# Moving a layer stack's prologue into the setup of a conditioned sequence kernel, with a shorter QR step and a tail spread over other phases

## The reference

```python
# L0: rotation
U, _ = jnp.linalg.qr(P)                      # P: 288 x 64
v = silu(cond) @ W.T + b                     # 2016 values a sample
A = skew matrix 64 x 64 from v;  R = expm(A)
z = einsum('btn,nd->btd', x, U)
x = x + einsum('btd,nd->btn', z @ R - z, U)
# L1, L2, L3: each with its own weights
s_a, c_a, g_a, s_f, c_f, g_f = split(silu(cond) @ W_ada + b_ada, 6)
h = layernorm(x) * (1 + c_a) + s_a
x = x + g_a * (softmax(q k^T / sqrt(18)) v @ W_proj + b_proj)   # 16 heads, q, k, v = h @ W_qkv + b_qkv
h = layernorm(x) * (1 + c_f) + s_f
x = x + g_f * (gelu(h @ W_fc1 + b_fc1) @ W_fc2 + b_fc2)         # 288 -> 1152 -> 288
```

## Time and profile before

| | us |
|---|---|
| median of three runs (lowest, highest) | 2118.55 (2117.92, 2121.7) |
| the profiled execution | 2125.66 |
| its span | 2123.9 |
| TensorE busy | 1966.4 (93%) |
| VectorE busy | 1224.8 (58%) |
| ScalarE busy | 1107.5 (52%) |
| GpSimd busy | 1015.8 (48%) |

### The profile page before, as it was taken

The page is one execution under the profiler, slowest core; times in us unless marked ns, Lnnn a source line. Parts: engine busy times, 40 slices in busy tenths (PEclk is TensorE's granted clock), DMA queues, the critical chain, the costliest instruction groups (busy, mean ns, idle before and its releaser), DMA issues. The chain is left out here.

```text
span 2123.9 us, 50051 instructions
## 1 busy us (share of the span) xinstructions
PE 1966.4 (93%) x16599; PEld 1746.1 (82%) x16599; DVE 1224.8 (58%) x2813; ACT 1107.5 (52%) x1906; POOL 1015.8 (48%) x1045
## 2 busy tenths in 40 slices
PE   4684599999999999999999999999999999999997
PEld 2553378998989988879989999888789899998986
DVE  7766375565655665574655556575656565565641
ACT  2222346656465564556465564654664655646552
POOL 2002164555545554655545545455645455454544
PEclk9887689999999999999999999999999999999998
DMA  6604243333233333343233333333432333333320
GB/s 167 160 13 142 83 135 107 95 89 99 80 108 91 93 95 95 111 131 100 80 104 88 98 99 84 99 88 93 144 96 81 103 88 99 99 83 100 86 80 25
DMA packets 138669, 207.65 MB, mean 98 GB/s; under 512 B 35204, under 2 KB 95778, under 8 KB 137518
## 3 DMA queue, kind: packets, MB, share of 16 engines
q1 hardware_dynamic: 111742, 171.06, 28.9%
q10 hardware_dynamic: 24192, 27.94, 4.7%
q0 software_dynamic: 2640, 7.44, 1.2%
HBM read 99.81 MB, written 20.82 MB: 57 GB/s over the span
## 5 line engine op out<-in xcount | busy, mean ns | idle before, releaser
L1968 DVE TENSOR_REDUCE maxima<-scores 128x4 f32<-128x1024 f32 x384 | 460.7, 1222 | 185.7 <-PE scores L1718 180.9
L1294 POOL TENSOR_TENSOR hidden<-g_full,hidden 128x512 fp32r<-128x512 f32 (+1 forms) x240 | 280.5, 1177 | 356.8 <-ACT hidden L1544 355.8
L1501 ACT ACTIVATE probs<-scores 128x1024 f32<-128x1024 f32 x384 | 383.2, 1026 | 95.2 <-PE pv_ps L1755 57.1
L1780 PE MATMUL mlp_ps<-h_mlp,w_up 128*128 128x256 f32 (+1 forms) x3024 | 405.6, 287 | 8.2 <-ACT hidden L1544 4.7
L1780 PEld LDWEIGHTS mlp_ps<-h_mlp,w_up 128*128 128x128 f32 (+1 forms) x3024 | 377.5, 191 | 42.0 <-issue 19.3
L1635 PE MATMUL mlp_ps<-w_down,hidden 128*128 128x288 f32 x2592 | 388.1, 294 | 0.0
L1635 PEld LDWEIGHTS mlp_ps<-w_down,hidden 128*128 128x128 f32 x2592 | 368.9, 188 | 18.5
L1718 PE MATMUL scores<-k_stack,q_stack 108*128 108x512 f32 x768 | 241.9, 407 | 22.4 <-DMA k_stack<-qk 18.4
L1741 PE MATMUL scores<-q_stack,k_stack 110*128 110x256 f32 x1536 | 246.5, 293 | 3.3 <-ACT probs L1501 2.0
L1741 PEld LDWEIGHTS scores<-q_stack,k_stack 110*128 110x128 f32 x1536 | 207.8, 191 | 32.1 <-issue 18.9
L1491 ACT ACTIVATE neg_max<-att_ps 16x256 fp32r<-16x256 f32 x48 | 18.0, 375 | 387.7 <-PE att_ps L1728 387.7
(11 more groups left out here) (221 smaller groups left out, 2865.9 us busy)
## 6 DMA issues: line engine op xcount, KB each, us to landing
q_stack<-qk SPq DMA_DIRECT2D x144, 180.0 KB
k_stack<-qk SPq DMA_DIRECT2D x288, 90.0 KB
inv_sum<-inv_scratch ACTq DMA_DIRECT2D x192, 128.0 KB, 2.7
k_stack<-qk SPq DMA_DIRECT2D x288, 54.0 KB
x_in<-out_x SPq DMA_DIRECT2D x48, 288.0 KB, 3.8
x_mid<-out_x SPq DMA_DIRECT2D x48, 288.0 KB, 4.2
out_x<-x_out SPq DMA_DIRECT2D x48, 288.0 KB, 3.1
q_stack<-qk SPq DMA_DIRECT2D x144, 72.0 KB
```

The source lines that it names most:

```text
L1294: tt(out, full, high.bitcast(F32), ALU.subtract).then_inc(signal, 1)
L1501: evict(probs[:, u % 4, :, :, :], scores[u % 2][:, :, :, :], ACT.Exp, scale=SCALE)\
L1780: last = mm(up_bank[n % 2][:, (m % 2) * T:(m % 2 + 1) * T], w[:, m * P:(m + 1) * P], h, start=count == 0, stop=count == 6)
L1968: nc.vector.tensor_reduce(out=maxima[:, :, :, u], in_=scores[u % 2][:, :, :, :], axis=AX.X, op=ALU.max).then_inc(s_max, 1)
```

## The change

The layers' tiles that the prologue writes are allocated first, and the setup (now called `prepare`) is called from within `layers` after them, with the tiles and semaphores handed over as `early`. What the prologue did is distributed over the setup: ScalarE fills `v_sb` and `k_stack` in phases 0 and 1 and rounds a third of `w_in` in each of phases 6, 7 and 8; GpSimd stages `w_in` after the skew loads; VectorE forms the low parts in the tail and the statistics and normalisation of sample 0, which it now adds into `x_in` directly, between the later adds. The wait for the stores moves from the end of the setup to the layers' SyncE program.

In the QR step `size` is gone: `pivot` is sign * alpha + norm with sign = +-0.5 in one instruction, with the scales of `mask`, the square roots and `norm_col` halved to fit. `turn` and `recip` share a semaphore, `factor` and `update` another. `recip` comes behind `update`. In a change, `spread` comes ahead of `norm_col`. Pair 1 goes into phase 3, pairs 2 and 3 into phase 4, one pair each into 5 to 8; the high powers go into phase 3 and the series and squarings forward; modulation set 0 goes into phase 8, set 1 to where set 0 was, set 2 behind the third pair's differences. The skew stores and loads are shared by SyncE and GpSimd, w_rot is loaded earlier, the constants and the first x group go over ScalarE's queue. Of `w_ada` two layers are held instead of three.

```diff
 (rotation_setup becomes prepare(nc, dram, keep, early))
-        SQUARES = {5: range(0, 6), 6: range(6, 15), 7: range(15, 24), 8: range(24, FILLS)}
-        PAIRS = {2: (0,), 4: (1, 2), 5: (3,), 6: (4,), 7: (5,), 8: (6,), PHASES: (7,)}
-        POWERS_AT, SERIES_AT = 3, 4
+        SQUARES = {5: range(0, 8), 6: range(8, 17), 7: range(17, 26), 8: range(26, FILLS)}
+        PAIRS = {2: (0,), 3: (1,), 4: (2, 3), 5: (4,), 6: (5,), 7: (6,), 8: (7,)}
+        POWERS_AT = 3
...
+        def skew_store(engine, q, half):
+            engine.wait_ge(s_v, q + 1)
+            for i in (2 * half, 2 * half + 1):
+                n = TILES * q + i
+                engine.dma_start(dram["v_scratch"][:, n * SKEW_COLS:(n + 1) * SKEW_COLS],
+                                 v_rot[32 * i:32 * i + B, q, :]).then_inc(s_v_st[half], 16)
+        def skew_load(engine, q, half):
+            for stored in s_v_st:
+                engine.wait_ge(stored, 32 * (q + 1))
+            rows = slice(R // 4 * q, R // 4 * (q + 1))
+            engine.dma_start(a_raw[half * R + rows.start:half * R + rows.stop, :, :], a_view[half, rows]).then_inc(s_a_ld[half], 16)
...
         @block.sync
+            for q in range(4):
+                skew_store(sp, q, 0)
+                skew_load(sp, q, 0)
+            sp.wait_ge(s_skew_ps, 4)
+            sp.wait_ge(s_a_ld[0], 64)
+            sp.wait_ge(s_a_ld[1], 64)
...
             for l in range(L):
+                if l == 2:
+                    sp.wait_ge(s_rows_ps, 1)
...
             sp.wait_ge(s_gates_st, 16 * TILES)
-            sp.wait_ge(s_out_st, 16 * B)
...
         @block.gpsimd
+            for q in range(4):
+                skew_store(pool, q, 1)
+                skew_load(pool, q, 1)
+            pool.wait_ge(s_x[2], 16)
+            for n in range(3):
+                early["stage"](pool, 0, n)
...
         @block.scalar
             for k in range(PHASES):
                 if k == 0:
+                    constant_stacks()
                     skew_out(0)
                 if k == 1:
+                    constant_rows()
                     skew_out(1)
                     skew_out(2)
+                    a, b = GROUPS[0]
+                    act.dma_start(x_all[:, a:b, :, :], dram["x"][a:b].rearrange("s p t c -> p s t c")).then_inc(s_x[0], 16)
...
+                if k in (6, 7, 8):
+                    high_weights(k - 6)
+                if k == LAST:
+                    mod_rows_out(0)
+                    mods_out(0)
                 if k < LAST:
                     norms(k)
...
         @block.vector
-                    V.tensor_scalar(size[h, i % 2:i % 2 + 1], alpha, -1.0, alpha, ALU.mult, ALU.max).then_inc(s_size, 1)
                 V.tensor_scalar(sign[h, n:n + 1], alpha, 0.0, 0.5, ALU.is_ge, ALU.subtract).then_inc(s_sign, 1)
...
-                V.tensor_tensor(pivot[h, n:n + 1], size[h, i % 2:i % 2 + 1], norm[h, n:n + 1], ALU.add).then_inc(s_pivot, 1)
+                dve.wait_ge(s_sign, n + 1)
+                V.scalar_tensor_tensor(out=pivot[h, n:n + 1], in0=alpha, scalar=sign[h, n:n + 1], in1=norm[h, n:n + 1],
+                                       op0=ALU.mult, op1=ALU.add).then_inc(s_pivot, 1)
...
-                dve.wait_ge(s_turn, n + 1)
-                dve.wait_ge(s_recip, n + 1)
+                dve.wait_ge(s_ratio, 2 * n + 2)
...
                 for i in range(WIDE):
-                    sign_and_size(k, i)
+                    sign_and_pivot(k, i)
...
-                    pivots(k, i)
                     turned(k, i)
-                    inverse_pivot(k, i)
                     if i:
                         update(k, i - 1)
+                    inverse_pivot(k, i)
                     factors(k, i)
...
                 whole_columns(k)
-                column_norms(k)
                 fill(k, GAP_A)
                 spread_rows(k + 1)
+                column_norms(k)
                 fill(k, GAP_B)
...
+            low_weights(0)
             dve.wait_ge(s_c_ps, 1)
...
+            rotated(0)
+            rotated(1)
+            for t in range(2):
+                V.bn_stats(out=stats[:, t, :], in_=x_in[:, t, :]).then_inc(early["s_stats"], 1)
+            rotated(2)
+            for t in range(2):
+                V.bn_aggr(out=mean_var[:, t, :], in_=stats[:, t, :]).then_inc(early["s_var"], 1)
+            for s in range(3, 8):
+                rotated(s)
+            (four tensor_scalar that write x_hat)
+            for s in range(8, B):
+                rotated(s)
...
 layers, block.sync
-            sp.dma_start(x_in[:, :, :], dram["out"][0]).then_inc(s_xin, 16)
+            sp.sem_inc(s_xin, 16)
+            sp.wait_ge(s_out_st, 16 * B)
+            sp.sem_inc(s_x_st, 16 * B)
...
 layers, block.vector, prologue
-                attention_norm(0)
-                x_hats(0, 0, x_in, s_xhat_a)
-                convert_weights(0, OF["w_in"], "qk")
-                convert_weights(0, OF["w_in"], "v")
-                (four tensor_scalar that write the last rows of k_stack)
                 for n in range(QK_USES):
                     qk_low(0, n)
```

477 lines of the change are left out of this document (247 added, 230 removed).

## The result

| | median us | lowest to highest | runs |
|---|---|---|---|
| before | 2119.69 | 2117.92 to 2121.7 | 4 |
| after | 2102.99 | 2097.45 to 2105.64 | 4 |

The ratio is 0.9918 (95% interval 0.9895 to 0.9940): 16.7 us faster, where 31.6 were forecast. 2087.0 and the whole range 2077 to 2098 were too low.

A forecast was written before the change was run, and what follows sets the result against it. It took a serial chain before the first query/key products as the bound. Gains of 15.4 (prologue), 2.5 (boundary), 2.8 (differences), 6.5 (tail) and 4.4 (QR) made 31.6, off the median 2118.55: 2087.0 us, range 2077 to 2098.

The forecast's parts named there:

- The start needs neither `both` nor its DMA wait: Start of the QR: a DMA wait of 1.04 us goes, gain 1.0.
- there the half-steps keep their instructions: Half-steps from 250 to 2110 us: instructions unchanged, so every edit lies in the first slices; no gain or loss counted.
- The slower rival: Last 47 half-steps grow from other tile places; from 0.67 us each all 31.6 is lost, at 1 us 2134; chance 0.04.
- I take 1.5 and 1.7: Ends of QR phases 3 and 4: TensorE late by 1.5 and 1.7 us, from ranges 0 to 3 and 0.5 to 3.5.
- 1.34 falling to 1.29: QR column time in us after the change, mean 1.31 against 1.25; loss 3.6 over nine phases.
- About 0.9 of barrier and branch stay: gain 2.5: Empty boundary between last add and layers: 3.4 us shrinks to about 0.9, gain 2.5 (1.5 to 2.8).
- Prologue 7.0: Layers' prologue up to the first query/key products: 7.0 us left of 22.4, gain 15.4 (13 to 16).
- differences 18.2: First difference matmul to last add: now 21.0 us, gain 2.8 (1.0 to 3.2) as one modulation set leaves.
- `c_mat` to the difference 10.5: Tail from `c_mat` to the first difference matmul: 10.5 us instead of 17.0, gain 6.5 (3.2 to 8.0).
- The tail's two prices: `c_mat` to the first difference: 13.8 us at TensorE's low clock, 9.0 at the high one.
- no stage is known to carry that difference: Profiled execution of before, 7.1 us above the 2118.55 median: excess assigned to no stage, so gain taken off the median.
- The skew rivals: Skew rows before `signed`: late by 4.9 us if GpSimd's backlog stays, 2091.9, chance 0.12; SyncE's first store behind weights, 2087 again.

The follow-up runs named there:

- start_order: Changed kernel with the loads of ident and both issued ahead of the first quarter of the weights; 2097.57 us, ratio 0.9895 to the kernel before.
- size_back: Changed kernel with size and a two-operand pivot back and the reciprocal ahead of update; result not the reference's; 2093.33 us, ratio 0.9887 to the kernel before.
- column: Changed kernel with the reciprocal issued ahead of update in every QR column, nothing else; 2097.04 us, ratio 0.9890 to the kernel before.
- after_again: The changed kernel, no edit, profiled and timed once more; 2102.77 us, ratio 0.9913 to the kernel before.
- best_nopairs: Changed kernel with small loads before the weights, overlapped skew trips and the reciprocal ahead of update; 2089.78 us, ratio 0.9855 to the kernel before.
- best_places: Changed kernel with small loads first, overlapped skew trips, reciprocal ahead of update, w_up and w_down allocated first; 2088.57 us, ratio 0.9852 to the kernel before.

## Why the prediction was wrong, and where it was right

Two steps missed by 5 us each: the start, and the half-steps taken as unchanged. The table has means of the two profiles of each kernel, since the first profile of before was 3.5 us longer than the second ahead of the products:

| stretch | before | after | gain | forecast | missed by |
|---|---|---|---|---|---|
| start to first `sign` | 7.3 | 11.8 | -4.5 | +1.0 | 5.5 |
| first `sign` to `c_mat` | 127.6 | 126.2 | +1.4 | +3.4 | 2.0 |
| `c_mat` to first difference | 15.9 | 10.3 | +5.6 | +6.5 | 0.9 |
| first difference to products | 46.8 | 27.9 | +18.9 | +20.7 | 1.8 |
| products to the end | 1922.8 | 1927.9 | -5.1 | 0 | 5.1 |
| sum | 2120.4 | 2104.1 | 16.3 | 31.6 | 15.3 |

**"The start needs neither `both` nor its DMA wait": gain 1.0.** This step failed first. The diff moved `unit` and `low` to ScalarE's queue and drew 1.15 MB of weights forward past them. I counted the wait that went and not the loads now ahead of those that VectorE still waits for. start_order shows it: with the weights behind the small loads the 4.5 lost become 0.9 gained.

**"there the half-steps keep their instructions".** I took their time as unchanged from that. The slower rival named the mechanism, longer half-steps from other places in memory, with "Nothing in the rows shows operand places to matter" against it, and priced it only from 0.67 us each. It came at a fifth of that, about 0.15 us in the first two layers and 0.07 later. Places were shown to give 0.04 to 0.06 us of it in every layer; the rest, most of it in the first two layers, is open. A comparison of spans hides it, since the irregular half-steps at a change of layer differ by 4 us between two runs of one kernel.

**"I take 1.5 and 1.7".** These are TensorE's delays at the ends of phases 3 and 4. The mechanism was right: almost no idle time before `norm_col` (0.2), and waits for TensorE before `spread`. The sizes were off. At the end of phase 4 it is 5.0 for 1.7, beyond my bound of 3.5, since both pairs ran at the low clock from end to end. Phase 3 had none of its 1.5, and phases 0, 1, 2 and 6 have waits of 2.1 in all that my sum hadn't. So 7.3 us of idle time are left where I counted 3.3. That the whole stretch misses by only 2.0 is a balance: the columns lost less than forecast.

**"1.34 falling to 1.29".** The QR column was right in kind, 1.33 falling to 1.26; seven distances of phase 1 sum to 0.25 more than before, not 0.4. The removed instruction was indeed hidden, and the reorder indeed cost (size_back, column).

**"About 0.9 of barrier and branch stay: gain 2.5".** No row stood behind the 0.9. 1.93 to 1.94 stayed in both profiles of the changed kernel; gain 1.5. It was the same, 1.91 to 1.94, in every other kernel with the change, so the barrier and branch cost twice my figure.

**Prologue 7.0, differences 18.2, `c_mat` to the difference 10.5.** Measured 7.3 and 7.8 in the two profiles, 18.4 and 10.3. The tail's two prices were met by other kernels, at 13.1 and 8.6. The gain there is 0.9 smaller than forecast only because before itself has two lengths, 17.0 and 14.7. Two sums are off by 0.1 each: the prologue's terms add up to 7.1, and 1.5 and 1.7 to 3.2 where 3.3 was taken off. The slips cancel.

**"no stage is known to carry that difference".** The second profile says which carry the 7.1 us: 3.5 before the products and 3.6 in the half-steps. The gains were worked out from rows that held the 3.5, and then taken off a median that doesn't: by so much the forecast was too large there. For the 3.6 in the half-steps taking the median was right.

**The skew rivals.** `signed` had no idle time, as forecast, but only because the start was late: with the start repaired it waited 2.1, and with the faster columns of size_back 1.3. Two misses covered each other.

## What to carry to other kernels

When a diff moves small loads to another queue, list by issue time everything large that is now issued ahead of the last of them, on any queue; the first wait of the program is for the last small one. On a chain of tiny VectorE instructions, put an independent instruction only where the queue would wait anyway. The update between a pivot and the reciprocal that waits for it cost 0.10 to 0.14 us, some sixty times, and putting it behind the reciprocal gave that back. And after a change of allocation compare one steady iteration, group by group, before believing that the untouched loop costs what it did.

## What the runs showed of the hardware

- A load of 16 KB issued 0.34 us behind 1.15 MB on another queue was there 7.2 and 7.9 us after its issue (after, after_again), and 2.2 us after it when the large one came later (start_order).
- Identical instructions with operands at other SBUF offsets: 540 products in 79.1 to 79.3 us instead of 78.3 and 78.4.
- TensorE's granted clock in a stretch isn't fixed by its instructions: the same phase took 14.7 us at 0.90 (best_nopairs) and 17.7 at 0.65 (best_places), and in two executions of the kernel before 18.8 at 0.89 and 17.3 at 1.00.
- A gain at a high clock in one stretch can stand beside a loss at a low one in another: against the changed kernel `column` was 5 us shorter in phase 4 (0.90 instead of 0.50) and 2.8 longer in the tail (0.61 instead of 0.83). Whether the first brings the second isn't shown.
